# Causal attention with a split-precision score product: half-array matmuls, two score units at a time, a shorter emptying of the sums, and more low halves on VectorE

## The reference: what is computed

```
xn = ln(x, g_norm)
q = (xn @ Wq).reshape(b, n, HEADS, DIM_HEAD)
k, v = split(xn @ Wkv)                  # one key head and one value head for all
k = concat([null_k, k]); v = concat([null_v, v])
q = l2norm(q) * q_scale; k = l2norm(k) * k_scale
sim = einsum('bhid,bjd->bhij', q, k) * 8 + bias      # bias[h, i - j], null bias for key 0
sim = where(causal and mask, sim, -max)
attn = softmax(sim)
out = ln((attn @ v) @ Wout, g_out)
x + dequant(round(quantized out)) @ ternary.T + f_bias
```

## Time and profile before

| | |
|---|---|
| median of three runs | 1657.63 us |
| profiled execution, its own time | 1657.8 us |
| its span in the trace | 1656.0 us |
| matmuls (PE) busy | 1508.3 us, 91% of the span |
| GpSimd busy | 1333.7 us, 81% |
| VectorE busy | 1325.0 us, 80% |
| ScalarE busy | 1076.6 us, 65% |

### The profile page before, as it was taken

The page is one execution under the profiler, slowest core; times in us unless marked ns, Lnnn a source line. Parts: engine busy times, 40 slices in busy tenths (PEclk is TensorE's granted clock), DMA queues, the critical chain, the costliest instruction groups (busy, mean ns, idle before and its releaser), DMA issues.

```text
span 1656.0 us, 39721 instructions
## 1 busy us (share of the span) xinstructions
PE 1508.3 (91%) x13844; PEld 987.3 (60%) x13844; DVE 1325.0 (80%) x2295; ACT 1076.6 (65%) x2168; POOL 1333.7 (81%) x924
## 2 busy tenths in 40 slices
PE   4988985999999999997998985999999999999797
PEld 2444443777777777775444442777777777777342
DVE  4456995798888888885898995888888888888597
ACT  4665664778778788787112664787787787787210
POOL 4664665999999999998564764999999999999563
PEclk9999996999999999999999997999999999999899
DMA  6004764111111111111796775112112012010596
GB/s 201 1 7 87 141 136 81 40 27 40 39 27 40 35 32 40 30 23 27 147 190 147 147 141 108 40 33 47 26 28 52 21 32 52 15 38 2 118 185 156
DMA packets 225620, 114.93 MB, mean 69 GB/s; under 512 B 193200, under 2 KB 193712, under 8 KB 225456
## 3 DMA queue, kind: packets, MB, share of 16 engines
q1 hardware_dynamic: 220864, 104.42, 30.6%
q10 hardware_dynamic: 4608, 8.39, 1.4%
HBM read 58.11 MB, written 8.54 MB: 40 GB/s over the span
## 4 chain that ended last, share of the span: by engine, by line
PE 53%; DVE 12%; issue 12%; DMA 6%; POOL 5%; ACT 2%; SPq 2%; DVEq 1%; ACTq 0%; POOLq 0%
PE ps L1300 23%; PE ps L1273 11%; PE ps L1276 10%; DVE work L1039 5%; PE ps L1339 5%; PE ps L1242 3%; DMA qo<-work 2%; DVE work L1067 2%; DMA work<-work 2%; SPq L445 1%; POOL work L589 1%; DMA tab<-bias_table 1%; POOL tab L566 1%; PE ps L1348 1%; DVE quot L996 1%
## 5 line engine op out<-in xcount | busy, mean ns | idle before, releaser
L576 POOL TENSOR_TENSOR work<-work 128x1024 f16<-128x1024 f32 (+2 forms) x576 | 978.1, 1730 | 54.6 <-ACT work L740 51.8
L1039 DVE SCALAR_TENSOR_TENSOR work<-ps,tab 128x1024 f32<-128x1024 f32 (+3 forms) x640 | 669.2, 1060 | 168.1 <-PE ps L1276 148.3
L740 ACT ACTIVATE work<-work 128x1024 f32<-128x1024 f32 (+3 forms) x640 | 578.1, 924 | 225.0 <-DVE work L1039 220.2
L1300 PEld LDWEIGHTS ps<-vals,work 128*128 128x128 bf16 (+1 forms) x8704 | 545.3, 98 | 115.8 <-POOL work L576 2.4
L1300 PE MATMUL ps<-vals,work 128*128 128x129 f16 x8704 | 600.6, 221 | 1.9 <-POOL work L576 1.8
L1273 PE MATMUL ps<-qo,kT 128*128 128x512 f16 (+3 forms) x1280 | 346.4, 353 | 36.7 <-DVE work L1039 21.8
L1276 PE MATMUL ps<-qo,kT 128*128 128x512 f16 (+3 forms) x1280 | 344.5, 351 | 0.0
L1276 PEld LDWEIGHTS ps<-qo,kT 128*128 128x128 f16 x1280 | 123.7, 99 | 119.2 <-issue 6.1
L1339 PE MATMUL ps<-wout,work 128*128 128x512 f16 x768 | 175.9, 388 | 15.6 <-DMA work<-work 15.6
L1242 PE MATMUL ps<-wq,tab 128*128 128x512 f16 x768 | 180.0, 385 | 9.7 <-DMA tab<-tab 9.5
L1339 PEld LDWEIGHTS ps<-wout,work 128*128 128x128 f16 x768 | 76.4, 100 | 110.3 <-DMA work<-work 16.0
(11 more groups left out here) (132 smaller groups left out, 1323.3 us busy)
## 6 DMA issues: line engine op xcount, KB each, us to landing
tab<-bias_table SPq DMA_DIRECT2D x64, 512.0 KB, 4.7
tab<-in_x SPq DMA_DIRECT2D x64, 256.0 KB, 3.1
out_x<-work ACTq DMA_DIRECT2D x32, 256.0 KB, 3.0
work<-in_L_cond_Wq SPq DMA_DIRECT2D x1, 2048.0 KB, 10.0
work<-in_L_cond_Wout SPq DMA_DIRECT2D x2, 1024.0 KB, 10.0
qo<-in_L_cond_w SPq DMA_DIRECT2D x1, 1024.0 KB, 7.3
work<-work SPq DMA_TRANSPOSE x64, 4.3
qo<-in_L_cond_b SPq DMA_DIRECT2D x2, 256.0 KB, 5.5
```

The costliest lines, as they stand in the source:

```text
L576: pool.tensor_tensor(low[:, k % LRING, :, c0:512], probs[:, r, :, c0:512], high[:, r, :, c0:512], ALU.subtract).then_inc(low_pool, 1)
L740: act.activation(probs[:, k % RING, :, c0:512], probs[:, k % RING, :, c0:512], ACT.Exp).then_inc(expd, 1)
L1039: dve.scalar_tensor_tensor(out=probs[:, k % RING, :, c0:512], in0=ps[:, 2 * (k % 2):2 * (k % 2) + 2, c0:512], scalar=SCORE, in1=tab[:, :, ...
L1300: last = pe.matmul(ps[:, sum_bank(i, q), (t % SUMS) * VS:(t % SUMS + 1) * VS], parts[:, rings[part], e, s * P:(s + 1) * P], vals[:, j, :], ...
```

## The change

There are four parts.

1. **Scores.** `score` is replaced by `score_two`, which computes two units. The product with `kT[:, 0]` stays as it is (`full`). The product with `kT[:, 1]` is done on 64 partitions only (`halves`): for the even head on partitions 0 to 63, for the odd head on 64 to 127, which is where the high half of each query lies, so that q_low·k_low is no longer computed. Three of the four half products are left. The order for a pair of units is full(k), halves(k), halves(k + 1), full(k + 1), with a wait for VectorE before halves(k + 1); both weigh slots come after.
2. **Values.** Their columns are now 64 high, ones, 64 low, instead of 64 high, 64 low, ones.
3. **Drains.** One addition takes the high columns and the denominator together (65 columns a sum), and a second adds the low columns. The addition of the denominators by itself is gone, and the reciprocal reads the eight denominators out of `o_part`.
4. **Low halves.** `DVE_LOW` has eight units instead of four, all of them 1024 columns wide (before, three were wide and one 256).

```
-DVE_LOW = (7, 11, 22, 27)
+DVE_LOW = (6, 9, 11, 16, 18, 22, 24, 29)
...
-        o_part = carve(work, SUMS, DH)
+        o_part = carve(work, 8, VW)
...
-                    dve.tensor_tensor(denom[:, i % 2, t0:t0 + n], acc[:, :, 2 * DH],
-                                      null_tmp[:, i % 2, t0:t0 + n, DH], ALU.add).then_inc(o_den, 1)
-                    dve.wait_ge(o_added, 3 * m + q + 6)
-                    dve.tensor_tensor(o_part[:, 0:n, :], acc[:, :, DH:2 * DH],
-                                      null_tmp[:, i % 2, t0:t0 + n, 0:DH], ALU.add).then_inc(o_low, 1)
+                    part = o_part[:, t0:t0 + n, :]
+                    dve.wait_ge(o_rec, m + 1)
+                    dve.wait_ge(o_added, 3 * m + q + 4)
+                    dve.tensor_tensor(part, acc[:, :, 0:VW], null_tmp[:, i % 2, t0:t0 + n, :], ALU.add).then_inc(o_part_in, 1)
+                    dve.wait_ge(o_part_in, 3 * m + q + 1)
+                    dve.tensor_tensor(o_sum[:, i % 2, t0:t0 + n, :], acc[:, :, VW:VS], part[:, :, 0:DH], ALU.add
+                                      ).then_inc(o_added, 1)
                     if q == 2:
-                        dve.wait_ge(o_den, 3 * m + 3)
-                        dve.reciprocal(rec[:, i % 2, :], denom[:, i % 2, :]).then_inc(o_rec, 1)
-                    dve.wait_ge(o_low, 3 * m + q + 1)
-                    dve.tensor_tensor(o_sum[:, i % 2, t0:t0 + n, :], acc[:, :, 0:DH], o_part[:, 0:n, :],
-                                      ALU.add).then_inc(o_added, 1)
+                        dve.reciprocal(rec[:, i % 2, :], o_part[:, :, DH]).then_inc(o_rec, 1)
...
+                def full(hp, k, start):
+                    i, j, c0 = unit(k)
+                    for e in range(2):
+                        last = pe.matmul(ps[:, 2 * (k % 2) + e, c0:512], kT[:, 0, j * P:(j + 1) * P],
+                                         qT[:, 2 * hp + e, 512 * i + c0:512 * i + 512], start=start, stop=not start)
+                    return last
+                def halves(hp, k, start):
+                    i, j, c0 = unit(k)
+                    for e in range(2):
+                        last = pe.matmul(ps[:, 2 * (k % 2) + e, c0:512], kT[e * DH:(e + 1) * DH, 1, j * P:(j + 1) * P],
+                                         qT[e * DH:(e + 1) * DH, 2 * hp + e, 512 * i + c0:512 * i + 512],
+                                         start=start, stop=not start, tile_position=(e * DH, 0))
+                    return last
+                def score_two(hp, k):
                     n = (b * HP + hp) * NU + k
-                    i, j, c0 = unit(k)
                     pe.wait_ge(biased, n - 1 + CB)
...
-                    last.then_inc(scored, 1)
+                    full(hp, k, True)
+                    halves(hp, k, False).then_inc(scored, 1)
+                    pe.wait_ge(biased, n + CB)
+                    halves(hp, k + 1, True)
+                    full(hp, k + 1, False).then_inc(scored, 1)
...
-                        for k in range(NU):
-                            score(hp, k)
+                        for k in range(0, NU, 2):
+                            score_two(hp, k)
                             weigh_slot(hp, k)
+                            weigh_slot(hp, k + 1)
```

More of the change, by code:

```diff
@@ L68 @@
 LRING = 8
-WORK = 16912
+WORK = 16928
 OUT_AT = 4096
@@ L233, in build @@
         rinv = sb("rinv", [P, 2, H + 1], F32)
-        denom = sb("denom", [P, 2, 8], F32)
         rec = sb("rec", [P, 2, 8], F32)
@@ L326, in build @@
             "b_qn", "b_kn", "b_hi", "b_khi", "b_lo", "b_klo", "b_turned", "b_cd", "b_snd", "b_pn"))
-        tab_ld, scored, biased, expd, pv_done, summed, null_ready, o_low, o_added, o_den, o_rec, o_stored = (
-            sem(n) for n in ("tab_ld", "scored", "biased", "expd", "pv_done", "summed", "null_ready", "o_low",
-                             "o_added", "o_den", "o_rec", "o_stored"))
+        tab_ld, scored, biased, expd, pv_done, summed, null_ready, o_part_in, o_added, o_rec, o_stored = (
+            sem(n) for n in ("tab_ld", "scored", "biased", "expd", "pv_done", "summed", "null_ready", "o_part_in",
+                             "o_added", "o_rec", "o_stored"))
         low_dve, low_pool, b_vh, b_vl = (sem(n) for n in ("low_dve", "low_pool", "b_vh", "b_vl"))
@@ L752, in store_o @@
                     m = (b * HP + hp) * NB + turn(i)
-                    act.wait_ge(o_rec, m + 1)
+                    act.wait_ge(o_rec, m + 2)
                     act.wait_ge(o_added, 3 * m + 3 + 6)
@@ L809, in _ @@
             for s, n in ((b_xn, 2), (b_qn, 2), (b_ss, 1),
-                         (b_vl, 1), (b_snd, 2), (b_rinv, 2), (biased, CB), (o_added, 6), (c_y1, 2), (c_fin, 2),
+                         (b_vl, 1), (b_snd, 2), (b_rinv, 2), (biased, CB), (o_added, 6), (o_rec, 1), (c_y1, 2), (c_fin, 2),
                          (c_zn, 2), (c_as, 2), (c_yq, 1)):
@@ L960, in ones @@
                     if t == 0:
-                        dve.tensor_scalar(vals[:, :, 2 * DH:VS].rearrange("p t o -> p (t o)"),
+                        dve.tensor_scalar(vals[:, :, DH:VW].rearrange("p t o -> p (t o)"),
                                           mask_r[:, b * NT:(b + 1) * NT], WSCALE, None, ALU.mult).then_inc(ones_set, 1)
@@ L1021, in b_values @@
                     dve.wait_ge(b_vh, g + 1 + 1)
-                    dve.scalar_tensor_tensor(out=vals[:, t, DH:2 * DH], in0=v,
+                    dve.scalar_tensor_tensor(out=vals[:, t, VW:VS], in0=v,
                                              scalar=mask_r[:, g:g + 1],
@@ L1266, in batch @@
                 project = [(b_project(1), 3), (b_project(2), 3), (b_turn_v, 4), (b_project(0), 3), (b_turn_k, 5)]
-                def score(hp, k):
+                def full(hp, k, start):
[12 more added lines that the diff above has]
+                def score_two(hp, k):
                     n = (b * HP + hp) * NU + k
-                    i, j, c0 = unit(k)
                     pe.wait_ge(biased, n - 1 + CB)
-                    for e in range(2):
-                        pe.matmul(ps[:, 2 * (k % 2) + e, c0:512], kT[:, 0, j * P:(j + 1) * P],
-                                  qT[:, 2 * hp + e, 512 * i + c0:512 * i + 512], start=True, stop=False)
-                    for e in range(2):
-                        last = pe.matmul(ps[:, 2 * (k % 2) + e, c0:512], kT[:, 1, j * P:(j + 1) * P],
-                                         qT[:, 2 * hp + e, 512 * i + c0:512 * i + 512], start=False, stop=True)
-                    last.then_inc(scored, 1)
+                    full(hp, k, True)
[3 more added lines that the diff above has]
+                    full(hp, k + 1, False).then_inc(scored, 1)
                 def weigh(hp, k, q):
```

## The result

The changed kernel takes 1797.53 us (median of 4 runs, 1795.59 to 1799.05) against 1660.1 us of the kernel before in the same series (4 runs): ratio 1.083, 95% interval 1.080 to 1.087, or +137 us. The forecast was 1721 us, with a range up to 1786. The direction was right, and so was VectorE as the engine whose reserve the change draws on; the size was not.

What follows compares the result with a forecast made beforehand. TensorE bounds the kernel now; VectorE was to become the bound. The larger work of each pair adds to 67.7, less 1.0 gives 66.7 us, 4.0 more a head pair; times 16 is 63, so 1721 us, range 1636 to 1786.

Steps and rivals of the forecast that it cites:

- What bounds the kernel: Attention head pair before the change: TensorE sets the pace, 60.6 of 62.75 us; VectorE's 8.7 us wait is the reserve.
- Scores: Score matmuls on TensorE: three half products, halves side by side, save 7.4 us a head pair; switches cost 0.15 a pair.
- (c): Rival on TensorE's scores: switches cost 0.5 us or the halves don't overlap, about 1785 us; chance 0.13.
- (d): Rival on TensorE's scores: both half-array matmuls share one queue, starts 0.217 us apart, no product saved; chance shared with (c).
- the prediction's own two lists: VectorE's and TensorE's work in us for each of 20 pairs of units; the larger of each adds up to 67.7.
- Drains: VectorE's drains of the sums: 0.66 us large, 0.60 small, 7.7 us a head pair against 8.2, a 0.5 us gain.
- the sum: Head pair length: larger of VectorE's and TensorE's work per pair of units, 67.7, less 1.0 for slack: 66.7 us.
- The forecast named the wait for `o_added` as harmless: In VectorE's drains: this wait reaches back a whole block and never binds, so no cost was counted.
- Low halves: VectorE's eight low halves: 1.14 to 1.97 us each because GpSimd's exclude them; 1.62 taken, 13.0 us a head pair.
- (a): Rival on the head pair's end: TensorE still sets it, VectorE fills its reserve, 60.9 us, 1628 in all; chance 0.20.
- (b): Rival on VectorE's low halves: they meet an idle GpSimd and cost 1.14 us each, 1667 us in all; chance 0.17.
- the signs that the prediction names: In a head pair: VectorE's share near 90%, eight GpSimd instructions near 2.9 us, TensorE's bias wait above 8 us.

Runs made afterwards that it cites:

- h1: Changed kernel with the first product of units 20, 22 and 34 repeated 2, 5 and 4 times more, ahead of TensorE's waits: 1793 us, ratio 1.083.

## Why the prediction was right in direction and wrong in size

*What bounds the kernel.* Right: VectorE's reserve was the thing drawn upon. Its busy time came out at 59.06 us a head pair for 59.9 forecast, GpSimd's at 53.6 for 57.2.

*Scores.* Right. The halves run side by side, and a pair of units pays 0.2 us for its two switches (0.15 taken, 0.5 the upper bound). Rivals (c) and (d) are out: both would show in those starts. Their price was also set too high by the prediction's own two lists: TensorE's work is the larger in nine of the 20 pairs, not eleven, and dear switches would add 3.4 us a head pair, not 4.

The Trainium skill, "TensorEngine Tiling (Array Packing)", section "Key Properties", says that a change of tiling mode drains TensorE; what the rows here show of it is 0.1 us a switch.

*Drains.* The size of the new drains was about right (a large drain holds VectorE for 0.65 us, from 591.21 to 591.86, where 0.66 was forecast; alone the new drains gain 7 us). The step that failed is in the sum, which treated a pair's work as a heap: "VectorE (biases, drains and low halves that stand there)". The drains of odd units stand between the two biases that TensorE waits for, and wait themselves for weighing that the new order put behind both units' scores. That costs 2.3 us a head pair in the changed kernel and 2.5 with four low halves, 41 and 43 us. The forecast named the wait for `o_added` as harmless, which it is, and did not look at `summed` and `pv_done` in the same row.

*Low halves.* The mean was forecast too high, 1.70 us for 1.51 to 1.55 measured. The cost of the exclusion, 3.4 us a head pair by the step from 1.14 to 1.62, was right with the drains where the change has them (3.5, 71.7 against 68.2), partly by luck since the mean was wrong, and too low with the odd drains later (4.9, 69.4 against 64.5). The mean hides that of the eight in a head pair one lasts 2.5 us, right ahead of a drain and a bias, and one 2.1. VectorE's own time is 64.5 - 60.4 = 4.1 us of the 9.1 that it adds.

*The clock.* The sum has no term for it: TensorE's 56.2 us are taken at 2.4 GHz in every pair of units, as in the rows of before. The runs showed falls to 1.2 GHz behind the new waits, 1.6 us for one of them in h1, and about 1.5 us a head pair in all as an estimate.

*The sum.* The forecast's 66.7 missed 5.0 us a head pair. How they divide depends on what is taken away first: 2.3 to 3.7 are the drains' place, 1.5 to 0.1 the exclusion, and 1.2 remain where both are gone (64.5 against 63.3). The clock's share is part of the first two. With the switches at their measured 0.2 us a pair the same sum of larger works gives 64.9 less 1.0 for that case, which explains half of the 1.2. But without any low half it gives 63.1 less 1.0, and 60.4 were measured: eight low halves of 1.14 us add 1.8 us by the sum and 4.1 in the runs. So a us of VectorE's work costs more than the larger of two sums says. Why is open.

*Rivals.* (a) failed: it was to decide where TensorE's wait stays below 3 us a head pair, and that wait is 10.3. (b) failed as a case: GpSimd was idle for 17 to 19 us a head pair and VectorE's low halves still met it in three of eight cases a head pair. With all of GpSimd's taken away, so that its condition holds fully, 1741 us were measured where (b) said 1667. Two of the signs that the prediction names did not come either: VectorE's share of a head pair is 82% instead of near 90%, and GpSimd shows five long instructions (2.5 to 2.9 us) in the second head pair above instead of eight.

## What to carry to other kernels

Where two engines hand banks to each other in program order, don't compare sums of work. Walk one pass of the waiting engine, and ask what stands between the two instructions that it needs; moving that behind them was worth 41 us here without touching any work. Price an instruction that excludes another engine at the place where it stands as well as by its mean: here one of 2.52 us ahead of a drain and a bias led to the 3.30 us wait. Where one engine's clock can fall, compare neighbouring head pairs of one run by their granted clock before calling a fall free. Before giving one more piece of work to an engine with idle time, look whether that idle time lies behind or ahead of the instruction that is waited for.

## What the runs showed of the hardware

- Two half-array matmuls of 64 rows with 512 columns, on different rows and different banks, run side by side: four in 0.43 us, after a switch of 0.1 us, and 0.1 us back.
- A low half on VectorE takes 1.22 us undisturbed and up to 2.98 beside GpSimd; with GpSimd's removed, none of 128 takes longer than 1.217 us.
- Where TensorE's clock fell to 1.2 GHz, 32 weighing matmuls took 3.45 and 3.67 us instead of 1.99. It fell there after waits of 3.30 us (changed kernel) and of 1.82 us with little work before (five low halves). After a wait of 1.89 us (h1) it stayed up in one head pair and fell in the next.
- A fall made a head pair 1.6 us longer where all else was the same (h1, 71.80 against 70.23). Keeping the clock up at one place by repeated work won 2.6 us there, of which 1.42 went to exclusion, and left the mean head pair at 71.8 against 71.7, with a fall at another place.
